# GRU products in four slot steps: 64-row products dealt to both row halves of TensorE, in place of 128-row products

## The reference, cut to what matters

```
for _ in range(3):
    sn = rmsnorm(slots, slot_norm_w);  q_proj = sn @ Wq.T
    scores = einsum('bkd,bmd->bkm', q_proj, k_proj) * SCALE
    attn = softmax(scores, axis=-2)                      # over the 1024 slots
    attn = attn / (sum(attn, axis=-1) + EPS)             # over the 64 inputs
    updates = einsum('bkm,bmd->bkd', attn, v_proj)
    gx = updates @ wih.T + bih;  gh = slots @ whh.T + bhh
    r = sigmoid(xr + hr);  z = sigmoid(xz + hz);  n = tanh(xn + r * hn)
    slots = (1 - z) * n + z * slots
```

## Time and profile before

| | |
|---|---|
| median of 3 runs | 555.71 us (554.62 to 558.26) |
| profiled execution | 557.2 us |
| its span | 555.4 us |
| mean granted TensorE clock | 0.972 |
| TensorE matmul busy | 507.8 us, 91% |
| VectorE busy | 438.9 us, 79% |
| ScalarE busy | 343.8 us, 62% |
| GpSimd busy | 250.5 us, 45% |

### The profile page before, as it was taken

How to read it: one execution, slowest core, us unless ns; L and a number is a source line. 1 busy time by engine, 2 the same in 40 slices (tenths; PEclk the granted TensorE clock), 3 DMA queues, 4 the chain that set the end, 5 groups by cost and what they waited for, 6 DMA issues and landing times.

```text
span 555.4 us, 7269 instructions
## 1 busy us (share of the span) xinstructions
PE 507.8 (91%) x2174; PEld 366.0 (66%) x2174; DVE 438.9 (79%) x794; ACT 343.8 (62%) x608; POOL 250.5 (45%) x217
## 2 busy tenths in 40 slices
PE   6999986978779999899999999999997999979992
PEld 2465552845557687488768867885885788767771
DVE  2899999997799477989967985897677567868783
ACT  3657539786598474667466656765663766557453
POOL 0133050400223256556935664574335156737776
PEclk9999999899898999999999999999997999989997
DMA  8960202210021032000000000002111136255752
GB/s 299 316 194 2 76 1 76 76 44 33 0 77 63 15 77 77 0 2 0 2 1 1 0 0 1 2 1 76 40 38 39 38 128 235 91 159 157 222 153 71
DMA packets 28101, 39.98 MB, mean 72 GB/s; under 512 B 7421, under 2 KB 19838, under 8 KB 27776
## 3 DMA queue, kind: packets, MB, share of 16 engines
q1 hardware_dynamic: 24656, 31.10, 18.0%
q0 software_dynamic: 3408, 8.43, 4.1%
HBM read 25.70 MB, written 16.83 MB: 77 GB/s over the span
## 4 chain that ended last, share of the span: by engine, by line
PE 51%; DVE 6%; issue 6%; POOL 4%; ACT 3%; DMA 1%; SPq 0%; POOLq 0%; ACTq 0%; DVEq 0%
PE psum L1452 35%; PE psum L1542 7%; PE psum L1255 3%; PE psum L1394 2%; PE psum L1513 2%; PE psum L1340 1%; POOL gru L1005 1%; DVE gru L1865 1%; POOL sorted_rows L1035 1%; DVE slots_full L1867 1%; POOL out L1043 1%; POOL slots_lo L1020 1%; PE psum L1352 1%; DVE gru L1845 1%; PE psum L1416 1%
## 5 line engine op out<-in xcount | busy, mean ns | idle before, releaser
L1452 PE MATMUL psum<-slots_hi,w_hh 128*128 128x512 f32 x560 | 181.5, 406 | 1.2 <-ACT gru L752 1.2
L1452 PEld LDWEIGHTS psum<-slots_hi,w_hh 128*128 128x128 f32 x560 | 104.5, 191 | 27.8 <-issue 4.2
L1005 POOL TENSOR_TENSOR gru<-slots_full,gru 128x512 f32<-128x512 f32 x43 | 65.7, 1529 | 111.8 <-ACT gru L758 111.8
L1452 PE MATMUL psum<-slots_lo,w_hh 128*128 128x512 f32 x280 | 112.0, 400 | 0.0
L1452 PE MATMUL psum<-at,v_ih_pair 128*128 128x512 f32 x288 | 91.4, 402 | 5.0 <-DVE at L1744 3.1
L758 ACT ACTIVATE gru<-gru,vec 128x512 f32<-128x512 f32 x48 | 34.7, 722 | 58.7 <-DVE gru L1845 58.6
L1452 PEld LDWEIGHTS psum<-at,v_ih_pair 128*128 128x128 f32 x288 | 53.7, 190 | 21.9 <-DVE at L1744 3.4
L1838 DVE SCALAR_TENSOR_TENSOR gru<-psum,vec,gru 128x512 f32<-128x512 f32 x48 | 35.9, 747 | 36.0 <-PE psum L1452 30.2
L1138 PE MATMUL psum<-early_hi,w_in 128*128 128x512 f32 x128 | 57.9, 611 | 5.3 <-DMA early_hi<-in_xT 5.2
L1452 PEld LDWEIGHTS psum<-slots_lo,w_hh 128*128 128x128 f32 x280 | 53.4, 191 | 12.9
L1865 DVE TENSOR_TENSOR gru<-gru 128x512 f32<-128x512 f32 x47 | 43.7, 929 | 7.2 <-POOL gru L1005 3.7
(11 more groups left out here) (249 smaller groups left out, 878.3 us busy)
## 6 DMA issues: line engine op xcount, KB each, us to landing
gathered<-sorted_rows SPq DMA_DIRECT2D x39, 129.0 KB, 2.5
x_scratch<-slots_full SPq DMA_DIRECT2D x8, 512.0 KB, 3.0
x_block<-x_scratch SPq DMA_DIRECT2D x8, 512.0 KB, 4.1
early_hi<-in_xT SPq DMA_DIRECT2D x3, 1024.0 KB, 5.4
x_tm<-in_x SPq DMA_DIRECT2D x4, 512.0 KB, 6.3
slots_full<-expert_plus SPq DMA_DIRECT2D x1, 2048.0 KB, 10.3
sorted_rows<-gru SPq DMA_DIRECT2D x1, 1032.0 KB, 11.7
early_hi<-in_xT SPq DMA_DIRECT2D x2, 512.0 KB, 4.6
```

The lines of the kernel that those rows point to most:

```text
L1005: pool.tensor_tensor(DF(u), full[:, c, seq(k, h), blk(j)], X(u), ALU.subtract).then_inc(d_pool, 1)
L1452: last = pe.matmul(psum[:, bank, :], w, d, start=start and i == 0, stop=stop and i == len(pairs) - 1, skip_group_check=begun or late)
```

## The change

Steps 1 to 4 (but unit 0 of step 1 and unit 7 of step 4) get `split_unit`. Each 128-row hidden product becomes two 64-row products, one in rows 0-63 (`lo`) and one in rows 64-127 (`hi`). An update by high weights becomes two as well; an update by low weights becomes one, only the high attention, which lies in one row half. A copy of it in the other half, `at_x`, lets that product be dealt to either half. `both` issues low and high products alternately, on different banks: while `lo` fills the r bank, `hi` finishes xn and z of the unit before, and so on. TensorE waits on its own signal `low_rows` before `hi` goes on in a bank that `lo` has filled. A unit has 45 products of 64 rows, 22 or 23 in each half. The copy is a transfer from on-chip memory to on-chip memory on SyncE's queue, one for each step and batch, waiting on `at_hi`. Mean squares and scores move into units 2 and 3 at "R", sums stay in unit 5 at "XN". On VectorE `spread_attention(k, 1)` moves ahead of `candidate(k, 2)`, and `tops(k+1)` behind `candidate(k, 3)`. ScalarE's and GpSimd's orders stay.

```diff
--- before.py
+++ after.py
@@ -165,6 +165,8 @@
         r_mm, hn_mm, xn_mm, z_mm = sem("r_mm"), sem("hn_mm"), sem("xn_mm"), sem("z_mm")
         r_act, z_act, n_act, t_dve, t2_dve = sem("r_act"), sem("z_act"), sem("n_act"), sem("t_dve"), sem("t2_dve")
         d_pool, e_dve, s_dve = sem("d_pool"), sem("e_dve"), sem("s_dve")
+        low_rows = sem("low_rows")
+        at_copied = [sem(f"at_copied_{h}") for h in range(2)]
         ss_mm, ss_ln, rstd_done = sem("ss_mm"), sem("ss_ln"), sem("rstd_done")
 
         rc_set, gw_in, g_mean, g_set = (
@@ -361,7 +363,8 @@
         wh = [sb2(f"w_hh{i}", [P, C, G3], F32R) for i in range(2)]
         fold = sb2("fold", [P, C, B, M])
         neg = sb2("neg", [P, P], F32R)
-        sb2("value_place", [P, 3 * C * B * M - P])
+        at_x = sb2("at_copy", [P, T], F32R)
+        sb2("value_place", [P, 3 * C * B * M - P - T])
         v_ih = [sb2(f"v_ih_pair{i}", [P, 2, 2, G3], F32R) for i in range(2)]
         brz = sb2("brz", [P, C, 2])
         def vp(w, b):
@@ -481,11 +484,28 @@
...
+    def copy_attention(k, h):
+
+        n = 2 * k + h
+        sp.wait_ge(at_hi, n + 1)
+        if k > 1:
+            sp.wait_ge(z_mm, U * (n - 1))
+        sp.dma_start(at_x[half(1 - h), :].bitcast(F32),
+                     at[n % 3][half(h), :].bitcast(F32)).then_inc(at_copied[h], 16)
+
+    copy_attention(1, 0)
     sp.dma_start(ew_dram, expertT).then_inc(plus_out, 16)
     sp.wait_ge(plus_out, 16)
+    copy_attention(1, 1)
+    copy_attention(2, 0)
     sp.wait_ge(corner_set, 1)
     for c in range(C):
         sp.dma_start(corners(ew_dram, c), corner[:, c], allow_slow_non_contiguous=True).then_inc(plus_out, 16)
+    copy_attention(2, 1)
+    for k in range(3, LAST):
+        for h in range(2):
+            copy_attention(k, h)
...
@@ -1495,6 +1515,142 @@
...
+    def both(lows, highs):
+
+        low = high = None
+        for i in range(max(len(lows), len(highs))):
+            if i < len(lows):
+                bank, w, d, start = lows[i]
+                low = pe.matmul(psum[:, bank, :], w, d, start=start, stop=False, skip_group_check=True)
+            if i < len(highs):
+                bank, w, d, start = highs[i]
+                high = pe.matmul(psum[:, bank, :], w, d, start=start, stop=True, skip_group_check=True)
+        return low, high
+
+    def split_unit(k, q, before, between=None, last=False):
+
+        h, j, c = place(q)
+        b, u = seq(k, h), QU * k + q
+        n_split = u - QU
+        between = between or {}
+        r, hn, z, a = r_bank(u), hn_bank(u), Z_B + u % 2, at[(2 * k + h) % 3]
+        lo, hi = half(0), half(1)
+        x_before, z_before = before
+
+        def cols(gate):
+            return slice(gate * D + c * P, gate * D + (c + 1) * P)
+
+        def hidden(bank, gate, rows):
+            return [(bank, wh[w][rows, i, cols(gate)], slots[d][rows, i, b, blk(j)],
+                     rows == lo and (i, w, d) == (0, 0, 0)) for i in range(C) for w, d in PASSES]
+
+        def update(bank, gate, rows, with_low):
+            first = [(bank, vp(0, b)[rows, cols(gate)], a[rows, blk(j)], rows == lo and gate == 2)]
+            high_part = a if rows == half(h) else at_x
+            return first + [(bank, vp(1, b)[rows, cols(gate)], high_part[rows, blk(j)], False)][0:with_low]
+
+        r_hid, hn_lo = hidden(r, 0, lo), hidden(hn, 2, lo)
+        r_hi, hn_hi = hidden(r, 0, hi) + update(r, 0, hi, 0), hidden(hn, 2, hi)
+        nz = len(z_before)
+        swapped = q == 0
+
+        if u == QU + U:
+            pe.wait_ge(x1_lo, 2 * H2)
+        if q == 0:
+            pe.wait_ge(s_hi, NB * (k - 1))
+            pe.wait_ge(s_lo, NB * (k - 1))
+        if swapped:
+            pe.wait_ge(r_act, u)
+            one, two = hn_lo, r_hid
+        else:
+            pe.wait_ge(t_dve, u - 1)
+            one, two = r_hid, hn_lo
+        if x_before:
+            pe.wait_ge(low_rows, 4 * n_split - 5)
+        low, high = both(one[0:2], x_before)
+        if x_before:
+            high.then_inc(xn_mm, 1)
+            pe.wait_ge(low_rows, 4 * n_split - 4)
+        low, high = both(one[2:], z_before[0:4])
+        if swapped:
+            low.then_inc(low_rows, 1)
+            pe.wait_ge(t_dve, u - 1)
+            low, high = both(two[0:nz - 4], z_before[4:])
+            two = two[nz - 4:]
+            high.then_inc(z_mm, 1)
+        if q % U == 0:
+            pe.wait_ge(at_lo, 2 * k + h + 1)
+        if q % U == 0 or u == QU + 1:
+            pe.wait_ge(at_copied[h], 16 * k)
+        if not swapped:
+            low, high = both(update(r, 0, lo, 1), z_before[4:6])
+            low.then_inc(low_rows, 1)
+            pe.wait_ge(r_act, u)
+            low, high = both(two[0:max(nz - 6, 1)], z_before[6:])
+            two = two[max(nz - 6, 1):]
+            if z_before:
+                high.then_inc(z_mm, 1)
+        if "R" in between:
+            between["R"]()
+
+        if swapped:
+            pe.wait_ge(low_rows, 4 * n_split - 3)
+            two = two + update(r, 0, lo, 1)
+            n = len(two)
+            low, high = both(two, hn_hi[0:n])
+            low.then_inc(low_rows, 1)
+            highs = hn_hi[n:]
+        else:
+            pe.wait_ge(low_rows, 4 * n_split - 3)
+            n = len(two)
+            low, high = both(two, r_hi[0:n])
+            low.then_inc(low_rows, 1)
+            highs = r_hi[n:]
+        if last:
+            low, high = both([], highs)
+            high.then_inc(r_mm, 1)
+            pe.wait_ge(low_rows, 4 * n_split - 2)
+            low, high = both([], hn_hi)
+            high.then_inc(hn_mm, 1)
+            pe.wait_ge(t2_dve, u)
+            for w in range(2):
+                mm = pe.matmul(psum[:, XN_B, :], vp(w, b)[:, cols(2)], a[:, blk(j)], start=w == 0,
+                               stop=w == 1, skip_group_check=True)
+            mm.then_inc(xn_mm, 1)
+            pe.wait_ge(z_act, u - 1)
+            pairs = [(wh[w][:, i, cols(1)], slots[d][:, i, b, blk(j)]) for i in range(C) for w, d in PASSES]
+            pairs = pairs + [(vp(w, b)[:, cols(1)], a[:, blk(j)]) for w in range(2)]
+            for i, (w, d) in enumerate(pairs):
+                mm = pe.matmul(psum[:, z, :], w, d, start=i == 0, stop=i == len(pairs) - 1,
+                               skip_group_check=True)
+            mm.then_inc(z_mm, 1)
+            return [], []
+        pe.wait_ge(t2_dve, u)
+        low, high = both(update(XN_B, 2, lo, 0), highs[0:1])
+        low.then_inc(low_rows, 1)
+        highs = highs[1:]
+        if swapped and not highs:
+            high.then_inc(hn_mm, 1)
+        if "XN" in between:
+            between["XN"]()
+        pe.wait_ge(z_act, u - 1)
+        z_lo = hidden(z, 1, lo) + update(z, 1, lo, u % 2)
+        n = len(highs)
+        low, high = both(z_lo[0:n], highs)
+        if swapped:
+            if n:
+                high.then_inc(hn_mm, 1)
+            pe.wait_ge(low_rows, 4 * n_split - 2)
+            low, high = both(z_lo[n:], r_hi)
+            high.then_inc(r_mm, 1)
+        else:
+            high.then_inc(r_mm, 1)
+            pe.wait_ge(low_rows, 4 * n_split - 2)
+            low, high = both(z_lo[n:], hn_hi)
+            high.then_inc(hn_mm, 1)
+        low.then_inc(low_rows, 1)
+        return update(XN_B, 2, hi, 1), hidden(z, 1, hi) + update(z, 1, hi, 1 - u % 2)
+
...
@@ -1552,17 +1708,20 @@
     unit(0, 5)
     unit(0, 6, {"XN": lambda: sums(1)})
     unit(0, 7)
+    rest = [], []
     for k in range(1, LAST):
-        unit(k, 0)
-        unit(k, 1)
-        unit(k, 2, {"HN": lambda: mean_squares(k + 1)})
-        scores(k + 1)
-        unit(k, 3)
-        unit(k, 4)
-        unit(k, 5, {"XN": lambda: sums(k + 1)})
-        unit(k, 6)
+        if k == 1:
+            unit(k, 0)
+        else:
+            rest = split_unit(k, 0, rest)
+        rest = split_unit(k, 1, rest)
+        rest = split_unit(k, 2, rest, {"R": lambda: mean_squares(k + 1)})
+        rest = split_unit(k, 3, rest, {"R": lambda: scores(k + 1)})
+        rest = split_unit(k, 4, rest)
+        rest = split_unit(k, 5, rest, {"XN": lambda: sums(k + 1)})
+        rest = split_unit(k, 6, rest, last=k + 2 == PAIRS)
         if k + 2 < PAIRS:
-            unit(k, 7)
+            rest = split_unit(k, 7, rest)
 
...
@@ -2154,11 +2313,11 @@
         settle(k, 0)
         if k == 1:
             lows(B - 1, H2 // 2, H2)
+        spread_attention(k, 1)
         candidate(k, 2)
-        spread_attention(k, 1)
         settle(k, 1)
+        candidate(k, 3)
         tops(k + 1)
-        candidate(k, 3)
         settle(k, 2)
         candidate(k, 4)
         weights(k + 1)
```

## The result

The changed kernel takes **573.3 us** (median of 4 runs, 571.1 to 576.2) against 556.7 for the kernel before: ratio 1.029, 95% interval 1.026 to 1.031. It is slower, as forecast, but by 16.6 us and not by 5.3; 573.3 lies just past the end of the range, 573. The profiled execution is its longest, 576.2, with a span of 574.4, 19.0 above that of before.

What follows compares the result with a forecast made beforehand. TensorE alone was taken to bound the kernel. Terms: -8.1 + 1.4 + 1.8 + 7.2 + 3.0 + 0.5 - 0.5 = +5.3 us, a forecast of 561.0 us on the median 555.71; range 547 to 573.

Steps and rivals of the forecast that it cites:

- the move of `tops`: On VectorE, `tops` behind `candidate(k, 3)`: claimed hidden, since it ends before r of unit 4 comes; no cost.
- the clock: TensorE's clock: the forecast had no term for it; the step before was read as running at full clock.
- Slots: TensorE, 30 split units: 685 slots of 0.2325 us in place of 720, as row halves run at once; -8.1 us.
- Cheaper: Rival: a slot of paired 64-row products costs 0.2146 us, as weight loads steal less; 551 us, chance 0.22.
- dearer slots: Rival: two weight loads in each slot make it 0.2525 us; 572 us, outer form 578; chance 0.19.
- no overlap: Rival: the row halves don't run at once, some 1,340 products in place of 720 slots; 705 us, chance 0.05.
- Tiling changes and self waits: TensorE: mode changes around four sums, +1.4 us; 15 waits of high products for low ones in a bank, +1.8 us.
- Sums: Sums in unit 5: r of unit 4 comes later, so TensorE waits 1.8 us for the weights, four times; +7.2 us.
- Mean squares: Mean squares wait for the last sum of squares, delayed by `settle` of unit 7; +0.5 us in three steps together.
- Copy: Unit 0 of the next step, slot 9: TensorE waits 1.0 us for attention and its copy, three times; +3.0 us.
- Step 1: Step 1: existing stops stay, its scores start 1.1 us later with seven slots more done (1.6); -0.5 us.
- no waits: Rival: waits at sums, copy and mean squares don't come, as engines catch up or overlap otherwise; 550.3 us, chance 0.10.

Runs made afterwards that it cites:

- s6: Changed kernel with sums in unit 6, r of units 7 and 5 earlier on ScalarE, copy wait in unit 1, attention and spread ahead of `high(k, 2)` on VectorE: 555.5 us.
- s7: Changed kernel with VectorE's old order: `tops` ahead of `candidate(k, 3)`, `spread_attention(k, 1)` behind `candidate(k, 2)`: 571.5 us.
- s2: Changed kernel with r of unit 7 directly behind the normaliser on ScalarE in steps 1 to 3: 571.4 us.
- s4: Changed kernel with sums at R of unit 6, r of unit 7 behind the normaliser and r of unit 5 ahead of squares on ScalarE: 557.4 us.
- s8: s6 with `high(k, 2)` behind `candidate(k, 7)` on VectorE: 554.3 us.
- b1: Kernel before, with sums between units 4 and 5 so that TensorE must wait for the weights; no 64-row products: 574.3 us.
- s1: Changed kernel with sums at R of unit 6 in place of XN of unit 5: 565.1 us.
- s9: s6, but each update by low weights is again two 64-row products, so the split without the saving: 563.9 us.

## Why the prediction was wrong, by its steps

Three steps failed: in unit 0 I asked for the attention and its copy and not for r of unit 7, I called the move of `tops` hidden, and the clock stood in the sum at nothing.

- **Slots, -8.1: right.** The row halves overlap and a slot is 0.23. "Cheaper" and "dearer slots" and "no overlap" fell with the first rows of the trace. That 572 was the figure of "dearer slots" is chance.
- **Tiling changes and self waits, +1.4 and +1.8: together somewhat high.** In s6 a step without its one wait (50.53 - 1.15) is 49.4, against 51.60 - 2.79 = 48.8 for the slots. The two so take 0.6 a step where I had 0.8. The way into the sums and out costs 0.41 over its slots in s6 (I had 0.34), and self waits show as one gap of 0.32 a step, 0.09 too long, where I had four of 0.12. The Trainium skill (TensorEngine Tiling (Array Packing), Key Properties) says that a change of tiling mode drains the engine; the rows fit it, with 0.33 from the first pair behind scores to the next where a slot is 0.23.
- **Sums, +7.2: right in place and mechanism, low in size.** Three waits were 2.1, that of step 4 about 2.9, 9.2 together. The chain that I named is right to the tenth: with VectorE's old order (s7) the waits are 1.8 each. What failed is "`tops` behind `candidate(k, 3)` is hidden". `tops` did end before r of unit 4 came (301.4 and 302.3), but I didn't look at what stands behind it: `settle` of unit 2 began later and held back `candidate` of unit 4, which is ahead of the weights. That is +2.0.
- **Mean squares, +0.5: nothing.** They start 0.31 us after the product ahead of them in steps 2 to 4, with no wait.
- **Copy, +3.0: the wait that I overlooked stood here.** At unit 0 I asked only for the attention and its copy. I had read that the unit begins with hn and overlooked what that does to the wait for the bank: r of unit 7 is wanted at slot 0 and no more at slot 8, and on ScalarE it stands behind the normaliser. That wait is 2.05 three times. The copy's own, about 1.2 at slot 9, was hidden behind it and came out in s2.
- **The clock, 0 in the sum and without a reason: the largest miss.** I priced each wait at its length. Six stretches of 3.4 us at half clock, at 1.5 to 1.6 each (s2's steps 54.4 and 52.8), are 9 us of the profiled execution. Of these the one in step 1 near 227 us, 1.6, is no cost that the new waits can be blamed for, since five of the other kernels have the same stops without it. I had the warning in front of me: the step before ran at 1.00 with no pause, and a forecast that puts two pauses of two microseconds into it has to ask what the clock does.
- **Step 1, -0.5: right in size.** Where the clock held (s4, s8), its scores come 1.0 us later from those of step 0 (45.1 against 44.1), with seven slots more done; I had 1.1. The second stop, which I had left ahead of the scores, now stands ahead of the mean squares, for GpSimd's sums of squares.

With r of unit 7 for the copy (+3.1), the sums as measured (+2.0) and the clock (+9) the forecast of +5.3 is 19.4, and without the mean squares and the excess of the self waits some 18; the profiled execution has 19.0. The rival "no waits" was the opposite of the truth. No rival held more waits than the forecast, and the range had no term for the clock.

What is not settled: why step 2 of the changed kernel has two falls of the clock and steps 3 and 4 one each, though all have the same two waits, and so what decides whether a wait of two microseconds is followed by one.

## What to carry to other kernels

When a product's order is changed, list for every bank the slot at which each wait now stands and read on the other engine's queue what is ahead of its releaser; a wait that moves from slot 8 to slot 0 is a change even if its text is the same. When an instruction is moved on a queue, look at what then stands behind it and who waits for that, and not only at when it ends itself. In this kernel, which TensorE bounds, a saving of products came only after the orders of ScalarE and VectorE had been moved with it: 8 us of saving made the kernel 17 us slower at first, and 3 us faster (557.5 to 554.3) after six moves of instructions and waits. And a wait put into a dense stream is priced with the clock behind it.

## What the runs showed of the hardware

- Products of 64 rows by 128 columns in the two row halves, on different banks, ran in pairs at the pace of one 128-row product, 0.23 us for 512 fp32r columns, with their starts mostly within 20 ns (at full clock 78% of the pairs in the changed kernel, 96% in s6). Two weight loads to a slot cost nothing more.
- After pauses of 2.0 to 2.9 us TensorE often went on at half clock for 3.4 us, sometimes for 6.8, also in a stream of 128-row products (b1); it cost 1.5 us for each 3.4. That is 16 of the 21 such waits in steps 1 to 4 of the changed kernel, s1, s2, s7 and b1, one of the four of 1.8 us in s7, and none of the 26 of 0.5 to 1.6 us that follow unit 2 of step 1 in s1 to s9. The Trainium skill (TensorE: Matmul & The Clock Gate, Part 1) gives 1.2 GHz for an idle array and 2.4 GHz for a busy one; the rows agree with these two levels (0.50, 1.00).
- A copy of 256 KB from on-chip to on-chip memory took 2.8 us from issue to landing (median of 8), next to 2.4 for 129 KB and 3.0 for 512 KB.
- The low spread on VectorE took 1.22 us whenever no GpSimd operation was under way as it began, and 2.17 to 2.34 when one was, in the kernel before as in all others. In s6 a GpSimd operation began 0.3 us after it: the spread still took 1.22, and that operation 2.08.
